# GpSimd's store of the LoRA inputs behind the round's scan loads, the first evacuation ahead of the router, the second half's statistics one round earlier

## What is computed

```python
# x (2, 1024, 2048), ctx (2, 2048, 2048), fp32
x = x + fake_quant(layernorm(x)) @ fake_quant(ctx)
y = layernorm(x)
probs = softmax(y @ W_router.T)              # 8 experts
topk_p, topk_i = top_k(probs, 2)             # weights of the two best, their sum scaled to 1
w = one_hot(topk_i) weighted by topk_p / sum(topk_p)
h = einsum('td,erd->ter', y, lora_A)         # rank 16 per expert, 128 columns in all
lora = einsum('ter,eor,te->to', h, lora_B, w) * 2
out = x + y @ W_base.T + b_base + lora       # W_base 2048 x 2048
```

## Time and profile before

| | us |
|---|---|
| median of 3 runs (lowest, highest) | 971.32 (968.44, 976.58) |
| the profiled execution | 970.02 |
| its span, first to last instruction | 968.2 |
| TensorE busy | 907.0 |
| VectorE busy | 611.8 |
| ScalarE busy | 371.3 |
| GpSimd busy | 144.9 |

### The profile page before, as it was taken

The page is one execution under the profiler, slowest core; times in us unless marked ns, Lnnn a source line. Parts: engine busy times, 40 slices in busy tenths (PEclk is TensorE's granted clock), DMA queues, the critical chain, the costliest instruction groups (busy, mean ns, idle before and its releaser), DMA issues.

```text
span 968.2 us, 12403 instructions
## 1 busy us (share of the span) xinstructions
PE 907.0 (94%) x4725; PEld 432.6 (45%) x4725; DVE 611.8 (63%) x955; ACT 371.3 (38%) x337; POOL 144.9 (15%) x191
## 2 busy tenths in 40 slices
PE   0599998999999999899999999999999999999997
PEld 0244443444445455354545455444444444444443
DVE  7678679853899864645565536699655365564511
ACT  3867436763455424332324232163213323133100
POOL 2536420422100101111111100010000000000000
PEclk9999999999999999899999999999999999999999
DMA  9999999989765878799999999956479879889621
GB/s 328 342 360 297 319 334 365 297 320 370 252 210 157 221 160 241 186 232 169 241 217 202 207 260 225 372 186 219 145 172 230 228 156 242 206 190 234 147 77 43
DMA packets 269310, 226.59 MB, mean 234 GB/s; under 512 B 221632, under 2 KB 222656, under 8 KB 265280
## 3 DMA queue, kind: packets, MB, share of 16 engines
q1 hardware_dynamic: 258880, 191.15, 73.0%
q0 software_dynamic: 10368, 34.61, 10.4%
HBM read 132.29 MB, written 39.94 MB: 178 GB/s over the span
## 4 chain that ended last, share of the span: by engine, by line
PE 71%; DMA 10%; DVE 9%; issue 3%; SPq 2%; ACT 2%; POOL 1%; DVEq 0%; POOLq 0%; ACTq 0%
PE PS L1644 50%; PE PS L1576 15%; PE PS L1661 4%; PE PS L1679 3%; DMA RJ<-wt 2%; DMA XR<-x 2%; DMA XV<-XU 2%; SPq L533 2%; DVE XR L1089 1%; DMA OQ<-x1d 1%; DVE NX L1270 1%; DVE ST L1012 1%; DMA x1d<-XR 1%; DVE ST L1096 1%; DVE OQ L1343 1%
## 5 line engine op out<-in xcount | busy, mean ns | idle before, releaser
L1644 PE MATMUL PS<-WS,XT 128*128 128x512 f16 x2736 | 599.1, 380 | 7.6 <-DVE OQ L1343 6.7
L1644 PEld LDWEIGHTS PS<-WS,XT 128*128 128x128 f16 x2736 | 267.6, 98 | 332.2 <-DVE OQ L1343 8.6
L1576 PE MATMUL PS<-QC,QT 128*128 128x512 bf16 x1024 | 225.4, 383 | 44.8 <-ACT QT L781 39.6
L1343 DVE SCALAR_TENSOR_TENSOR OQ<-PS,ZI,OQ 128x512 f32<-128x512 f32 x124 | 90.9, 748 | 166.4 <-PE PS L1644 89.4
L1576 PEld LDWEIGHTS PS<-QC,QT 128*128 128x128 bf16 x1024 | 100.3, 99 | 168.8 <-issue 47.1
L823 ACT ACTIVATE NX<-Yb 128x1024 f16<-128x1024 f32 x52 | 54.8, 1053 | 113.4 <-DMA XT<-NX 57.6
L708 POOL TENSOR_SCALAR CU<-CS,K,S 128x1024 uint8<-128x1024 f32 x64 | 79.2, 1239 | 122.2 <-DMA CS<-ctx 107.2
L727 POOL DMA_DIRECT2D out<-OQ x64 | 34.6, 541 | 392.5 <-DVE OQ L1343 384.2
L1270 DVE TENSOR_TENSOR NX<-Yb,NX 128x1024 f16<-128x1024 f32 x52 | 63.4, 1219 | 34.8 <-ACT NX L823 34.7
L791 ACT ACTIVATE QC<-CU,K 128x1024 bf16<-128x1024 uint8 x64 | 70.0, 1137 | 13.0 <-POOL CU L708 9.7
L1270 DVE TENSOR_TENSOR NX<-Ya,NX 128x1024 f16<-128x1024 f32 x40 | 47.9, 1221 | 36.4 <-ACT NX L823 36.0
(11 more groups left out here) (135 smaller groups left out, 468.9 us busy)
## 6 DMA issues: line engine op xcount, KB each, us to landing
CS<-ctx SPq DMA_DIRECT2D x64, 512.0 KB, 6.3
OQ<-x1d SPq DMA_DIRECT2D x64, 256.0 KB, 4.4
out<-OQ POOLq DMA_DIRECT2D x64, 256.0 KB, 5.3
Ya<-x1d SPq DMA_DIRECT2D x14, 1024.0 KB, 6.6
Yb<-x1d SPq DMA_DIRECT2D x14, 1024.0 KB, 7.4
XR<-x SPq DMA_DIRECT2D x9, 1024.0 KB, 8.6
x1d<-XR SPq DMA_DIRECT2D x16, 512.0 KB, 6.7
FB<-wt SPq DMA_DIRECT2D x8, 1024.0 KB, 9.8
```

Of the source, the lines that this page charges most:

```text
L1343: stt(OQ[ob][:, :], PS[:, bank(i, b), :], ZI[:, half(i), 1:2].bitcast(F32), OQ[ob][:, :], ALU.mult, ALU.add).then_inc(s_rd, 1)
L1576: ins = pe.matmul(PS[:, 2 * (t % 4) + c, :], QT[t][:, kt, :], QC[h][:, kt, c * CH:(c + 1) * CH], start=(kt == 0), stop=(kt == KT - 1))
L1644: ins = pe.matmul(PS[:, bank(i, b), :], XT[SLOT[i, j]][:, xi, kt, :], WS[half(i)][blk][:, :, kt // 2, wi, kt % 2, :], start=(fresh and n = ...
```

## The change

Four edits, none of which adds or takes away an instruction:

1. GpSimd: in each round the store of the LoRA inputs (`hstore`) is moved from between the second and third scan load to behind the last scan load, ahead of the out stores. It matters in rounds 1 to 5; rounds 0 and 7 have no scan loads and round 6 has two, so their order stays.
2. VectorE, rounds 2 to 5: r1 goes straight behind `rmax`; then come `clo(q, 2)` and S1, then the router, then S3 and `clo(q, 3)`. Before, the order was rmax, router, r1, clo(q, 2), S1, S3, clo(q, 3).
3. VectorE: `rstd2(1)` is moved from round 2 (ahead of its rmax) to round 1 (ahead of its rmax).
4. VectorE, round 1: the three bias adds of round 2 go behind the last four evacuations of round 1; SyncE loads OQ (1,0) of round 2 ahead of the two Y loads of pair 3, not behind them.

```diff
@@ SyncE
             ctrans(2, 4)
+            oload(2, (1, 0))
             yload(3, 0)
             yload(3, 1)
-            oload(2, (1, 0))
             ctrans(2, 5)
@@ GpSimd
             for i in range(NI):
                 for j in range(1, 7):
-                    if j == 3 and i < NPAIR:
-                        hstore(i)
                     if (i, j) in SCAN_AT:
                         raw_for_scale(SCAN_AT[i, j])
+                if i < NPAIR:
+                    hstore(i)
@@ VectorE, round 1
             clo(2, 1)
+            rstd2(1)
             rmax(1)
...
             clo(2, 6)
-            badd(2, (0, 0))
-            badd(2, (0, 1))
-            badd(2, (1, 0))
             ev(1, "r3")
             ev(1, "r4")
             ev(1, "r5")
             ev(1, "r6")
+            badd(2, (0, 0))
+            badd(2, (0, 1))
+            badd(2, (1, 0))
@@ VectorE, dve_round
-                if i == 2:
-                    rstd2(1)
                 if i < NPAIR:
                     rmax(i)
-                    router(i)
                     ev(i, "r1")
                 if q is not None:
                     clo(q, 2)
                     csum(q, S1)
+                if i < NPAIR:
+                    router(i)
+                if q is not None:
                     csum(q, S3)
                     clo(q, 3)
```

## The result

The changed kernel took 968.81 us (median of 20 executions), the kernel before 976.38 us (20 executions, among them the three of the table above). The ratio is 0.9929, with a 95% interval of 0.9904 to 0.9954: 6.9 us less, between 4.5 and 9.4 (the medians differ by 7.6). The forecast was 961.9 us, 9.4 less. In absolute time the result lies 0.8 us above the top of the range, because the three executions of before that the sum was hung on (971.3) were low: over 20 the median is 5.1 us higher. (Two executions of the changed kernel, 1089 and 1985 us, were disturbed.)

A forecast was written before the change was run, and what follows sets the result against it. TensorE was taken as the bound, busy 907.0 of 968.2 us, so only its holes could be won: 9.7 us less 0.3 lost is 9.4. From the 971.3 us median this gave 961.9 us, range 958.0 to 968.0.

The forecast's parts named there:

- The base: Whole kernel: the 9.4 us gain was subtracted from 971.3 us, the median of the runs shown, giving 961.9 us.
- The holes as fixed numbers: TensorE, rounds 2 to 5: holes of 3.96, 0.32, 0.89, 1.92 us plus 2.65 of low clock, together 9.7 us.
- L22 (2.24 us to go): L22 of rounds 3 and 5: waits of 0.32 and 1.92 us vanish once the store stands behind the scans.
- r3a stands behind P5 alone: VectorE, rounds 3 and 5: with scans earlier, r3a waits only for P5, some 5 us ahead of L22.
- The late router: Rounds 2 to 5: SyncE's LoRA transpose waits for the later router, 1.0 us in round 4; cost 0 to 0.5, hidden.
- rival 3: Late router, SyncE's queue and next transposes slip together; from about 5 us each costs TensorE one: 978 us, chance 0.04.
- P6 (7.5 us to statistics, router and low clock): P6 of rounds 2 and 4: earlier r1 and moved statistics remove 3.96 and 0.89 us, plus 2.65 of low clock.
- Round 6 (0.3 us): Round 6: r1 behind the Yb load comes too late for P6; 0.3 us lost, between the ends 0 and 1.9.
- Rounds 7 and 8 shift as one: Rounds 7 and 8: full of VectorE work, but TensorE's banks release its first splits, so the gain carries through.
- Rival 2: Rounds 7 and 8: base loads do not come forward and 3.3 us of the gain return: 965.2 us, chance 0.10.
- Rival 1: Moved scans slow Yb load and transposes, keeping r1 of rounds 4, 6 and the L22s late: 964.7 us, chance 0.18.
- Signs of being wrong: P6 of round 4 or 6 waiting behind Yb, SyncE waiting several us for the router, or grown 674 to 685 holes.

The follow-up runs named there:

- router behind r1: The changed kernel with VectorE's router directly behind r1 in rounds 2 to 5, ahead of lower half 2 and S1: 961.2 us, ratio to before 0.984.
- halved scans: The changed kernel with every scan load and absolute sum cut to 256 of 512 columns: 963.8 us, ratio to before 0.986.
- router behind r1, store back: The changed kernel with the router directly behind r1 and GpSimd's LoRA store back between second and third scan load: 975.9 us, ratio to before 0.998.
- bias adds back: The changed kernel with round 2's bias adds and OQ (1,0) load put back to their old places: 971.4 us, ratio to before 0.994.
- round 8 above: The changed kernel with router directly behind r1 and, in round 8, r2 ahead of r4 and the (1,1) bias add: 962.9 us, ratio to before 0.984.
- store put back: The changed kernel with only GpSimd's LoRA store put back between second and third scan load: 984.5 us, ratio to before 1.008.

## Why the prediction was wrong, step by step

- **The base (the step that failed for the time).** The forecast time was a difference taken from a median of three. Its own 9.4 us from the 20-execution median of 976.4 would have been 967.0 us, within the range and 1.8 from the result. This alone carried the time out of the range.
- **The holes as fixed numbers.** 9.7 us were added from one execution, "all that these rounds can give". Three profiles of before lose 10.4, 14.2 and 14.9 us against 178.1. By the profiles' means the change wins 191.3 - 180.7 = 10.6 us in rounds 2 to 5 and 693.9 - 684.0 = 9.9 in the second part; by time it wins 6.9 (4.5 to 9.4). The difference lies ahead of the second part, which started at 271.8 us in the mean of before's three profiles and at 275.8 in the changed kernel's two. Nothing that the change does reaches the first product, and fourteen profiles of kernels whose first product is the changed one's start the second part anywhere from 270.5 to 278.0, so I take it as scatter; its cause stays open.
- **L22 (2.24 us to go).** The step that failed here is "r3a stands behind P5 alone". The bound was worked out for the lower half of index 4. r3a also stands behind index 5, whose buffer comes free when the transposes of index 2 have landed, and these wait for P6's end and for SyncE. Before, the scan hid this; after, 1.53 + 0.30 and 2.21 + 0.35 us remain.
- **The late router ("0 to 0.5 us, hidden").** The 1.0 us of SyncE's standing was worked out for round 4 alone. It was 2.1 us in round 2, and P6's end did not hide it: the transposes went out 2.5 us behind that end. Against the router behind r1 this costs 7.6 us between the medians, and 3.0 to 3.9 us of second part between the profiles; the rest of the 7.6 is not traced. This is rival 3's mechanism at a smaller price: it does not need 5 us of lateness, since the 11.4 us from issue to ScalarE's start had already used up L22's slack.
- **P6 (7.5 us to statistics, router and low clock).** The holes went, but the cause was named too near. The store's move alone, priced at 2.2 us for L22 and at nothing for P6, takes 3.96 + 2.65 + 0.89 down to 2.6 us in four small waits and gives the whole of the change's gain; r1's move with the store back takes nothing off the time. What made r1 late in round 2 was ScalarE, late from the scans, ahead of rmax. That the size of the forecast (9.4 us) came out close to the profiles' 9.9 is therefore luck: a part credited with 7.5 us gave next to none on balance, and one credited with 2.2 gave all.
- **Round 6 (0.3 us).** Right: 0.41 and 0.27.
- **Rounds 7 and 8 shift as one.** Right: 1.81, 0.94 and 0.16 us in all the kernels whose VectorE order there is unchanged. Rival 2 did not come.
- **Rival 1.** Half right: halved scans take the L22 holes away, so load on the transfers counts; but with the scans forward and the router early there is no such hole, so it does not by itself.
- **Signs of being wrong.** Two came, both small: P6 of round 6 waited 0.41 us behind the Yb load, and SyncE stood 2.1 us for the router in round 2.

## What to carry over

In a queue that goes strictly in order, look first at what stands ahead of the wait that every round repeats: one 0.5 us store behind a long wait cost 8.0 us here, and 13 to 15 us once r1 stood ahead of the router; r1's place was worth nothing with the store in the way and 7.2 us without it. Moving a consumer forward is paid by whoever was moved behind it: follow that one to its own queue (router, LoRA transpose, transposes, lower half, evacuation) before calling it hidden. And hang a sum on more than one profile when holes come from landings: the kernel before, whose executions scatter by 1%, had other holes in each of three profiles.

## What the runs showed of the hardware

- The two transposes of index 2 in round 2 landed (median of the two, from issue) in 9.5 us in the changed kernel, 6.9 with the router behind r1, 5.9 with halved scans and 4.0 with the three OQ loads (768 KB) behind them. ScalarE could go on 11.4, 8.3, 7.0 and 6.7 us after the first was issued. SyncE issued the transposes and OQ loads, GpSimd the scan and the store of the same moment. The Trainium skill, "DMA: Bandwidth & Descriptors", section "Issuing engines are not separate DMA queues", says that DMAs which different engines start run on the same 16 DMA engines and interleave; these numbers agree. Traffic does not set it alone: the first two kernels move the same bytes.
- TensorE's granted clock fell from its upper to its lower level (2.4 to 1.2 GHz) behind idle stretches of 2.56, 3.31, 3.96 and 5.67 us, seen as 1.7 to 2.7 us more for the 96 matmuls behind them; the hole of 2.56 us thus cost 2.56 + 1.69 = 4.25 us. The length of the stretch does not tell it by itself. Nine matmuls kept their 2.10 us, and the granted clock 1.00, behind 2.21 us (changed kernel, second profile), 2.66 (router behind r1, store back) and 3.22 (bias adds back), and the 96 of round 0 their 20.88 us behind 2.50 (changed kernel, second profile); but nine took 2.87 behind 2.23 us (round 8 above), 3.79 behind 2.43 (store put back) and 3.70 behind 3.73.
